# One stage for layer 0: attention and experts under a table of steps for each engine, batch statistics from the inputs' products, gate exponentials in pairs

## What is computed

```python
def _branch(x, W, gamma, beta):
    h = jnp.einsum('bnd,ed->bne', x, W)
    hf = h.reshape(B * N, D)
    mean = jnp.mean(hf, axis=0)
    var = jnp.var(hf, axis=0)
    hn = (hf - mean) * jax.lax.rsqrt(var + BN_EPS) * gamma + beta
    return jax.nn.sigmoid(4.0 * (hn - V_TH))
q, k, v = _branch(x, Wq, gq, bq), _branch(x, Wk, gk, bk), _branch(x, Wv, gv, bv)
qk = _heads(q * k) * scale
vv = jnp.einsum('bhnd,bhne->bhde', v_h, v_h)
out = jnp.einsum('bhnd,bhde->bhne', qk, vv)     # then @ Wp.T + bp, added to x

h = x @ Wm + bm                                 # experts, on the normalised sum
logits = t @ expert_emb                         # t: h in 8 head slices of 16
w = jax.nn.softmax(logits, axis=-1)
topw, topi = jax.lax.top_k(w, K)
hmid = jax.nn.gelu(jnp.einsum('td,edi->tei', t, W1) + b1, approximate=False)
eo = jnp.einsum('tei,eio->teo', hmid, W2) + b2  # gated, summed, @ Wo + bo, added to x
```

## Time and profile before

| what | before |
|---|---|
| median of 3 runs | 1503.66 us (1502.87 to 1508.42) |
| profiled execution | 1503.48 us, of which the traced span is 1501.6 us |
| PE busy | 1387.8 us, 92% of the span |
| DVE busy | 1205.5 us, 80% |
| ACT busy | 1106.0 us, 74% |
| POOL busy | 281.9 us, 19% |
| mean granted clock of TensorE | 0.971 of full speed |
| PE's share of the chain that ended last | 72% (DVE 15%, ACT 5%, POOL 4%) |

### The profile page before, as it was taken

How to read it: one execution, slowest core, us unless ns; L and a number is a source line. 1 busy time by engine, 2 the same in 40 slices (tenths; PEclk the granted TensorE clock), 3 DMA queues, 4 the chain that set the end, 5 groups by cost and what they waited for, 6 DMA issues and landing times.

```text
span 1501.6 us, 23168 instructions
## 1 busy us (share of the span) xinstructions
PE 1387.8 (92%) x8350; PEld 645.1 (43%) x8387; DVE 1205.5 (80%) x2596; ACT 1106.0 (74%) x2054; POOL 281.9 (19%) x238
## 2 busy tenths in 40 slices
PE   6568999999989978899999999999999999999995
PEld 3441222222248856233333333333333335565884
DVE  8776777777368889998787998888788768999994
ACT  4537999999858622788787888888888886887554
POOL 4100000000013341222111111101111012234454
PEclk9889999999989988999999999999999999999997
DMA  3045665555310101000000000000000000000000
GB/s 100 4 118 126 150 150 151 148 151 146 126 58 1 73 1 52 20 1 1 1 1 1 1 1 1 1 1 1 1 0 1 1 28 1 1 8 8 8 15 22
DMA packets 43602, 63.11 MB, mean 42 GB/s; under 512 B 5344, under 2 KB 25056, under 8 KB 43104
## 3 DMA queue, kind: packets, MB, share of 16 engines
q1 hardware_dynamic: 43488, 61.62, 14.8%
HBM read 54.27 MB, written 7.34 MB: 41 GB/s over the span
## 4 chain that ended last, share of the span: by engine, by line
PE 72%; DVE 15%; ACT 5%; POOL 4%; issue 3%; DMA 1%; POOLq 0%; SPq 0%; ACTq 0%; DVEq 0%
PE ps L2011 16%; PE ps L2001 12%; PE ps L277 7%; PE ps L554 7%; PE ps L1980 6%; PE ps L2021 4%; PE ps L1990 3%; DVE p6ac L2499 2%; PE ps L563 2%; PE ps L700 2%; PE ps L2438 2%; POOL WA L2191 1%; PE ps L2401 1%; PE ps L191 1%; POOL WA L2195 1%
## 5 line engine op out<-in xcount | busy, mean ns | idle before, releaser
L2094 ACT ACTIVATE p4E<-ps,p4mx,p4sc 128x512 f32<-128x512 f32 x512 | 393.6, 773 | 107.7 <-DVE p4mx L2057 107.1
L2055 DVE TENSOR_REDUCE p4mx<-ps 128x2 f32<-128x1024 f32 x256 | 312.8, 1222 | 86.1 <-PE ps L2001 83.4
L2011 PE MATMUL ps<-p4E,p4vn 128*64 128x512 f32 x1024 | 247.5, 605 | 0.2 <-POOL p4vn L2116 0.2
L2001 PE MATMUL ps<-p4T 64*128 64x512 f16 x1536 | 209.9, 380 | 5.0 <-ACT p4E L2094 4.9
L2116 POOL TENSOR_TENSOR p4vn<-p4v,p4zs 128x512 f32<-128x512 f32 x64 | 66.7, 1042 | 480.5 <-DVE p4zs L2060 480.5
L167 POOL TENSOR_TENSOR rs<-rs,cst 128x4 f32<-128x4 f32 x58 | 63.1, 1088 | 456.6 <-DVE rs L161 456.1
L286 ACT ACTIVATE p1g<-ps,WB 128x1024 f32<-128x1024 f32 x128 | 137.5, 1135 | 13.0 <-PE ps L277 12.3
L277 PE MATMUL ps<-p1R,p1w1s 128*128 128x512 bf16 x475 | 136.7, 383 | 9.1 <-issue 3.3
L586 DVE SCALAR_TENSOR_TENSOR p1Pb<-ps,WB,p1sh 128x512 f32<-128x512 f32 x128 | 94.7, 748 | 57.7 <-PE ps L554 57.6
L554 PE MATMUL ps<-p1g,WB 128*32 128x512 f32 x512 | 136.3, 608 | 0.0
L554 PE MATMUL ps<-xn,WB 128*32 128x512 f32 x256 | 135.4, 612 | 0.3 <-DVE p1Pb L586 0.3
(11 more groups left out here) (349 smaller groups left out, 2500.1 us busy)
## 6 DMA issues: line engine op xcount, KB each, us to landing
p1sh<-gscr SPq DMA_DIRECT2D x128, 256.0 KB
p1R<-tscr SPq DMA_DIRECT2D x64, 128.0 KB, 4.9
tscr<-p1tp SPq DMA_DIRECT2D x24, 128.0 KB, 2.3
WA<-in_w SPq DMA_DIRECT2D x1, 2632.0 KB, 9.8
WB<-in_w SPq DMA_DIRECT2D x1, 2560.0 KB, 9.3
X<-in_x SPq DMA_DIRECT2D x8, 256.0 KB, 5.5
gscr<-p1gT SPq DMA_DIRECT2D x8, 256.0 KB, 5.1
out<-X SPq DMA_DIRECT2D x8, 256.0 KB, 2.3
```

The source lines that it names most:

```text
L2001: y = p.e.matmul(ps[:, at + hh, :], t[rows, q, 128 * j:128 * j + 128], t[rows, 2 + r, :], start=o == 0, stop=o == 2)
L2011: t = p.e.matmul(ps[64 * hh:64 * hh + 64, self.bank["ctx", n], :], vn[n % 2][:, j, 64 * hh:64 * hh + 64], E[2 * (n % 3) + hh][:, j, :], st ...
L2055: v.e.tensor_reduce(m, ps[:, at:at + 2, :], AX, ALU.max).then_inc(v.own.h, v.one())
L2094: a.e.activation(self.E[2 * (n % 3) + hh][:, j, :], ps[:, at + hh, :], ACT.Exp, bias=self.mx[i][:, j, hh:hh + 1], scale=pre.sc[:, 1, 0:1], ...
```

## The change

`Attention0` and `Mixture` become one class, `Layer0`.

**Order.** Each engine has a string of letters, one letter for a step (531 letters for PE). For PE: a transposes of the attention's rows, b products for the statistics, c one projection, d and e the statistics' two products, f transposes of v, g v times v, h times Wp, i q*k times that; j, k, l, m the preparation's transposes, Wm, logits and gate transposes; n an `mm1` pair, o a combination, p a sum, q the product with Wo, r the next layer's first transposes. PSUM banks are dealt in two rings, five banks to the attention (0, 1, 2, 3, 6), two to the rest (4, 5); GELU's pairs of banks stay. The first `mm1` waits until the attention's last block has been added.

**Statistics.** The first pass makes no projections to keep. For each block PE adds up the products of the normalised rows with themselves (128x128) and with a column of 1/4096; mean and variance of all three projections follow from these sums and the weights, in three small steps. Projections are made once, later, and ACT's sigmoid reads them straight from PSUM; the full-size buffers, the copies of line 804 and the statistics of lines 756 and 759 go. Row normalisation in this pass moves to ACT (`ln_scaled`, four 128x128 activations for a block) with a shift computed on DVE, and the copy to `xT` moves from ACT to DVE; the copy of the transposed v moves from DVE to ACT.

**Exponentials.** They are taken for block 0, then blocks 1 and 2, 3 and 4, 5 and 6, then 7, with two buffers each for logits and gates.

```diff
-class Mixture:
+class Layer0:
...
+    EXPS = ((0,), (1, 2), (3, 4), (5, 6), (7,))
...
+    ORDER = {
+        "tensor": (
+            "abbacbacbababbbdeafaaccccfcgghfhiicccccfcjgkhfgihlciccccjgckfhgfihclicgcccfhgimhinnnnjnnoonnnkononnnlonnonnnoo"
...
+        "sync": (
+            "IIV566666666V66I666V66666I666666VI6666V666666I666666VI6666V666666I6666V6666666666"),
+    }
...
+        spare = k.W[0][:, 646:646 + 4608]
+        self.H = [[col(1024 * w + 512 * i) for i in range(2)] for w in range(3)]
...
+        for ring, among in enumerate(((0, 1, 2, 3, 6), (4, 5))):
+            uses = [u for what, x in self.order("tensor") for u in self.banks(what, x) if self.ring(u) == ring]
+            n = len(among)
+            self.bank |= {u: among[i % n] for i, u in enumerate(uses)}
+            self.last |= {u: uses[i - n] for i, u in enumerate(uses) if i >= n}
...
+        return 0 if use[0] in ("turn0", "proj", "vT", "vv", "M", "y0") else 1
...
+            elif what == "gram":
+                p.wait_ge(k.sem("A", "row"), 4 * x + 4)
+                p.wait_ge(k.sem("nth"), 1)
+                for j in range(4):
+                    r, end = k.xn[:, 4 * x + j, :], x == NB - 1 and j == 3
+                    p.e.matmul(ps[:, 7, 0:128], r, r, start=x + j == 0, stop=end, skip_group_check=True)
+                    t = p.e.matmul(ps[:, 7, 128:129], r, self.nth[:, :], start=False, stop=end, skip_group_check=True)
+                t.then_inc(k.sem("gram").h, 1)
+            elif what == "cov":
+                p.wait_ge(k.sem("w", 0), 16)
+                p.wait_ge(k.sem("summed"), 1)
+                p.e.matmul(ps[:, 7, 0:384], self.gram, k.W[0][:, 0:384], start=True, stop=True).then_inc(k.sem("cov").h, 1)
+            elif what == "moments":
+                p.wait_ge(k.sem("wt"), 1)
+                for w in range(3):
+                    p.e.matmul(ps[:, 7, 384 + w:385 + w], self.wt[:, cols(w)], self.nth[:, :], start=True, stop=True)
+                    t = p.e.matmul(ps[:, 7, 387 + w:388 + w], k.W[0][:, cols(w)], self.mu[:, :], start=True, stop=True)
+                t.then_inc(k.sem("moments").h, 1)
+            elif what == "proj":
+                b, w = x
+                p.wait_ge(k.sem("w", 0), 16)
+                p.wait_ge(k.sem("A", "xT"), b + 1)
+                p.wait_ge(k.sem(("vT", "y0", "qk")[w]), b - 1)
+                self.released(p, (what, x))
+                p.e.matmul(ps[:, bank[what, x], :], W0(("wv", "wq", "wk")[w]), k.xT[:, 512 * b:512 * b + 512], start=True, stop=True).then_inc(k.sem("proj").h, 1)
...
+                p.wait_ge(k.sem("x0"), NB)
...
+            elif what == "rows0":
+                k.ln_shift(v, "A", x, x)
+            elif what == "turn0":
+                v.wait_ge(k.sem("A", "turned"), x + 1)
+                v.e.tensor_copy(k.xT[:, 512 * x:512 * x + 512], ps[:, bank[what, x], :]).then_inc(k.sem("A", "xT").h, 1)
+            elif what == "gram out":
+                v.wait_ge(k.sem("gram"), NB)
+                v.e.tensor_copy(self.gram, ps[:, 7, 0:128]).then_inc(v.own.h, v.one())
+                v.e.tensor_copy(self.mu[:, :], ps[:, 7, 128:129]).then_inc(k.sem("summed").h, 1)
+            elif what == "wt":
+                v.wait_ge(k.sem("cov"), 1)
+                v.e.tensor_tensor(self.wt, ps[:, 7, 0:384], k.W[0][:, 0:384], ALU.mult).then_inc(k.sem("wt").h, 1)
+            elif what == "coef 0":
+                v.wait_ge(k.sem("moments"), 1)
+                v.e.tensor_copy(mom[:, :], ps[:, 7, 384:390]).then_inc(v.own.h, v.one())
+                v.wait_ge(v.own, v.n)
+                v.e.tensor_tensor(sc[:, 1, :], mom[:, 3:6], mom[:, 3:6], ALU.mult).then_inc(v.own.h, v.one())
+                v.wait_ge(v.own, v.n)
+                v.e.tensor_tensor(sc[:, 0, :], mom[:, 0:3], sc[:, 1, :], ALU.subtract).then_inc(v.own.h, v.one())
+                v.wait_ge(v.own, v.n)
+                v.e.tensor_scalar(sc[:, 0, :], sc[:, 0, :], 0.0, EPS, ALU.max, ALU.add).then_inc(k.sem("bnvar").h, 1)
...
+            if what == "rows0":
+                a.wait_ge(k.sem("A", "shift"), x + 1)
+                k.ln_scaled(a, "A", x, 4 * x)
+            elif what == "sig":
+                b, s = x
+                w = (2, 0, 1)[s]
+                a.wait_ge(k.sem("bncoef"), 1)
+                a.wait_ge(k.sem("proj"), 3 * b + s + 1)
+                a.wait_ge(k.sem(("vT", "y0", "qk")[s]), b - 1)
+                a.e.activation(self.H[s][b % 2], ps[:, bank["proj", x], :], ACT.Sigmoid, bias=sc[:, 4, w:w + 1], scale=sc[:, 2, w:w + 1]).then_inc(k.sem("sig").h, 1)
+            elif what == "vt":
+                a.wait_ge(k.sem("vT"), x + 1)
+                a.wait_ge(k.sem("vv"), x - 1)
+                a.e.copy(self.vt[x % 2], ps[:, bank["vT", x], :]).then_inc(k.sem("vt").h, 1)
+            elif what == "exp":
+                for b in self.EXPS[x]:
+                    Df, Ef = (t[b % 2].rearrange("p a c -> p (a c)") for t in (self.D, self.E))
+                    a.wait_ge(k.sem("D"), b + 1)
+                    a.wait_ge(k.sem("gateT"), b - 1)
+                    a.e.activation(Ef, Df, ACT.Exp).then_inc(k.sem("exp1").h, 1)
...
-            for w in range(3):
-                v.wait_ge(k.sem("h"), 3 * b + w + 1)
-                v.e.bn_stats(self.bst[:, w, 6 * b:6 * b + 6], H[w][:, 512 * b:512 * b + 512]).then_inc(v.own.h, v.one())
-        v.wait_ge(v.own, v.n)
-        for w in range(3):
-            v.e.bn_aggr(bmv[:, w, :], self.bst[:, w, :]).then_inc(v.own.h, v.one())
-        v.wait_ge(v.own, v.n)
...
-        for q in range(4):
-            for w in (2, 0, 1):
-                h = H[w][:, 1024 * q:1024 * q + 1024]
-                a.e.activation(h, h, ACT.Sigmoid, bias=sc[:, 4, w:w + 1], scale=sc[:, 2, w:w + 1]).then_inc(k.sem("sig").h, 1)
...
+            elif what == "load":
+                sp.wait_ge(k.sem("x0"), NB)
+                k.load_w(sp, 2)
...
```

854 lines of the change are left out of this document (372 added, 482 removed), and 31 rows, old and new, of tables (AGAIN, KINDS).

## The result

The changed kernel takes **1509.71 us** (median, 1505.87 to 1513.06) against 1503.64 us for the kernel before: a ratio of 1.0037, with a 95% interval of 1.0027 to 1.0046. The forecast was 1480 us in a range of 1470 to 1497. The slowdown of 0.4% is small, but clear of the noise. The profiled execution (1508.79 us) has a span of 1506.7 us. Layer 1 starts at 438.23 us of it, against 432.35 before, and what follows is as long as it was (1506.7 - 438.23 = 1068.5, before 1069.3). So in these two executions all of it happened in layer 0.

What follows compares the result with a forecast made beforehand. PE was taken to bound the steady stream, leaving gains only in the first 182 us: first sigmoid 32.5, first `mm1` 86.0, block 0's product 141, plus 268 gives layer 1 at 409, 23.3 us earlier: 1480 us, range 1470 to 1497.

Steps and rivals of the forecast that it cites:

- The bound: Layer 0: a new order can win only in the first 182 us; PE sets the steady stream's pace, busy 241 of 250 us.
- the rest: Stream from block 0's product with Wo to layer 1: 269.4 us of work times 250.3/251.6, so 268 us.
- the first lands at about 6 us and DVE comes to it at 8.5: nothing added: First gate load at the stream's start: lands before DVE needs it, costing 0, or 3 us if that cover goes.
- PE's work hides them, so I count 0: ACT's table switches in the stream: pairing exponentials drops three of eight, 2 x 1.28 us each, counted as no gain.
- First pass: Start of layer 0 up to the first sigmoid: ends at 32.5 in place of 46.31, 13.8 us earlier.
- Second pass: First sigmoid to first `mm1`: 46.7 us of PE work, plus 3 for waits and 2.5 for the clock; `mm1` at 86.0.
- The rival of the cold clock: Second pass at 1.2 GHz: its 46.7 us take 93.4, layer 1 20.8 us later, 1524 us; chance 0.05.
- The start: First `mm1` to the end of block 0's product with Wo: 52.8 us of PE work plus 2 of waits, 55, ending at 141.
- the starved stream: Stream: combinations and preparation share two banks, late gatings hold PE and the clock falls; 3 us gain left, 1500; chance 0.09.
- DVE keeps its old share: From 32.5 us to block 0's product: DVE stays 76% busy, layer 1 only 9.4 us earlier, 1494 us; chance 0.17.

Runs made afterwards that it cites:

- the first run: PE's two waits ahead of a combination (gate load, and the sum that frees the buffer) taken out of the changed kernel: 1500.12 us, ratio 0.9975.
- either edit alone: Changed kernel with PE's two waits before a combination removed (1500.12 us), or with four gate loads moved ahead of the preparations' round trips on SP (1502.19 us).
- the mended table: Changed kernel without PE's two waits, four gate loads ahead of round trips on SP, block 7's exponential moved beside a sum: 1495.98 us, ratio 0.9943.

## Why the prediction was wrong, step by step

**The bound.** "What a new order can win lies in the first 182 us, and what it cannot win is PE's own work" is contradicted by no run: an undisturbed block takes 39.9 to 40.6 us in every kernel. But it left out what an order can lose: from block 0's product on I gave the new table the old table's idle time, 250.3/251.6, as if that were the kernel's and not the order's. This is the largest failed step: the rest took 286.3 us in place of 268. PE's busy time there is 267.3. (The share itself was a little off: with 0.89 us for a product the old order's sum is 251.1 and not 251.6, which is half a us of the forecast.)

**The diff, read for edits and not for waits.** My parts do not name the two `wait_ge` lines in front of the combination. I placed the gate loads' lateness on DVE ("the first lands at about 6 us and DVE comes to it at 8.5: nothing added"). They stood on PE, in order, and cost 9.6 us with what hangs on them (the first run). The landing was wrong as well: the gates' own way from the copy at 88.54, a write of 4.68 us, an issue of 0.72 and a load of 5.09, ends at 99.7, 8.3 us into the stream and not 6.

**SP.** I costed no step of SP's table. One reordering there is worth 8.8 us at L1, 8.3 of the stream. I had asked what the loads wait for at the start of the stream, and not again at each block.

**Exponentials.** "PE's work hides them, so I count 0" was false in size, both ways. In this table each absence of ACT without a sum beside it costs 1.8 to 3.0 us of PE's waiting, so those that stayed cost some 7 us (2.35 and 2.74, and 0.9 for each of two beside sums), and pairing saves three more, 8.6 us. In the old order the eight absences cost PE no wait over 0.4 us but the first (2.77 us, at 110.59). "ACT is busy 36.9 of 40.6" hides this: the average says that ACT has room. For how long it can be away depends on how much work PE can do without it, and the kernel has three pairs of PSUM banks for `mm1` to run ahead in. The price of a switch itself was right: 1.28 us, with the exponential right behind it, as the changed kernel's ACT shows:

```profile
112.07 1.28 ACT L716 ACT_TABLE_LOAD   x1
113.36 1.15 ACT L716 ACTIVATE WB<-WB 128x512 f32<-128x512 f32 x2
114.54 1.28 ACT L723 ACT_TABLE_LOAD   x1
115.83 2.12 ACT L723 ACTIVATE xT<-ps,WB 128x1024 f32<-128x1024 f32 x2
```

The Trainium skill ("ScalarE: Activation LUTs", What ACT_TABLE_LOAD costs) gives the load the same 1283 ns and adds some 1380 ns of drain for every switch; the rows show no such time between the instructions, so here the measurement decides.

**First pass.** Forecast 32.5, measured 39.45. Two terms of the sum were mis-sized. PE: I gave the one-column products 0.22 each and let PE have slack. A tile (both products) costs 0.45 us warm, but 0.86 for the first ten us, so PE works without a gap from 9.73 to 33.3; I had bounded the products at half clock, and taken a lower value. DVE: 26.6 in my sum, 31.2 with PE out of the way (the run without the one-column products), where the trace shows no wait of DVE from 8 us on. So of the 6.7 us by which the copy comes late, 4.6 are DVE's own list and 2.1 PE's. DVE's W1 steps there are 7.6 us against my 5.3, and three of its seven small steps of L163 took 1.0 to 1.1 us in place of 0.17. Why the same small step costs six times as much in places, no run settles. In the change DVE also waits 2.7 us for PE's transposes. The chain from the copy to the sigmoid was right: 5.9 forecast, 39.45 - 33.31 = 6.1.

**Second pass.** Forecast 53.5 us from sigmoid to first `mm1`, measured 52.0. PE 48.25 busy (46.7 and the cold clock), short waits of 0.45 to 0.78. This was right, by its own steps. The rival of the cold clock needed more than half the pass cold; the clock is 0.95.

**The start.** Forecast 55, measured 60.4; without PE's waits 57.8. To my 2 us of waits come the load of the GELU table, which the early pairs had hidden before (1.68 us), and the first pair of exponentials (2.35).

**The rivals.** The nearest in time is the starved stream (1500, chance 0.09; 9.7 us under the result): it said that the start would be earlier and the stream would give it back, with the clock falling behind each wait. Its cause, the two shared banks, was not the one in the change: no wait over 0.25 us for DVE is among the stream's, apart from block ends. It came up only in experiments (the runs with two loads in front, the moved exponential, the moved gating). What gave it back were gates and ACT, on the same path. My rival on the slower side was the wrong mechanism. That DVE keeps its old share did not happen.

Of the 29.2 us at layer 1's start between forecast and result, 7.0 are the first pass, -1.5 the second, 5.4 the start, 18.3 the rest (about 1 us of the last belongs to the start, since the forecast counted block 0's product there). Of the last two, 8 to 11 are gates and PE's waits, shown by either edit alone; 2 to 4 more go with all edits together. Some 8 to 11 us are left in every order tried: the best stream takes 331.2 us, the mended table's 334.1, against my 323, in pieces of 0.8 to 2.8 us that my prices do not have. Nine of the experiments' kernels beat both the kernel before and the change. Two of them end the account: the old order behind the new attention, 0.9951 (0.9932 to 0.9971), and the mended table, 0.9943 (0.9927 to 0.9959). So the new attention and its statistics, under the old order of the stream, are worth half a per cent, and the table of the stream as it stood cost nearly one.

## What to carry to other kernels

Where an order is written out by hand, its losses are its own: price each engine's and each queue's table at each block, SP's too, and don't carry an old table's idle share over. Look in a diff for every added wait and ask what stands behind it on its engine; here the same wait cost some 10 us on the engine that feeds everybody (PE) and little on the one that consumes the data (DVE), as long as DVE's delay did not hold a bank that PE needed. When an engine must be away (a table load), what it costs is decided by the work that its neighbours have in stock at that moment and not by its busy share: here 0.9 us beside two sums, 1.8 to 3.0 without.
